# Vision tower on one core: edge filter in row tiles of 64 with both kernels side by side, halo rows split on GpSimd and stacked by transfers, eight banks in turn

## The chip, the cores and the metric

One core of one Trainium2 chip. The metric is the device time of one execution in microseconds, the median of several runs; lower is better. The kernel before takes 307.37 us (median of 3 runs, 306.79 to 307.87).

TensorE multiplies matrices into eight PSUM banks (PE in the profile, its weight loads PEld), VectorE (DVE), ScalarE (ACT) and GpSimd (POOL) work on elements, and SyncE (SP) issues transfers, as the other engines can. Each engine works through its own instructions in order and waits on semaphores for the others.

## The reference

Eight images of 3 x 256 x 256 become a tower of one layer. All is fp32.

```
gray  = einsum('bchw,c->bhw', x, (0.2989, 0.587, 0.114))
edges = conv3x3(gray, [scharr, scharr.T])            # SAME, zeros outside
h     = abs(edges).sum(over the two kernels) / 2     # [8, 256 rows, 256 columns]
n     = layernorm(h)
q, k, v = n @ Wq + bq, n @ Wk + bk, n @ Wv + bv      # 16 heads of 16
q, k  = q @ Wp, k @ Wp                               # per head
h     = h + softmax(q k' / 4) v                      # per image and head, 256 x 256 scores
n     = layernorm(h) * gamma + beta
h     = h + 0.5 * (silu(n @ w1 + b1) @ w2 + b2)      # w1, w2 dequantised from int32 with scales
```

## The kernel before

Every fp32 product is made of three fp32r matmuls: each operand is split into a high and a low part, and high x high, low x high and high x low are summed in a PSUM bank. So each stage has a copy that makes the high part (mostly ScalarE) and a subtraction that makes the low part (VectorE or GpSimd).

The images are worked on in four pairs (p = 0 to 3). An image's 256 rows are two tiles t of 128 rows. For a pair the tower does this:

- `gray_scale`, `gray_add`, `gray_high`, `gray_low`: the weighted sum of the three colours of image b and its two parts.
- `tok(p, i)`, i = 0 to 3: the edges of row tile `i // 2` with kernel `i % 2`, as matmuls of a banded 128x128 matrix with the gray rows, three for each of the three column shifts: nine of 512 columns (two images side by side). A tenth adds the halo: rows that belong to the neighbouring tile, kept for all images in `halo`.
- `edge`: ScalarE takes the absolute value of each bank, one kernel to `absd`, one to `hid`. `edges` on VectorE adds the two, `tok_moments` takes mean and variance, `tok_rstd` on GpSimd the inverse deviation, `tok_normalise` makes `xn`.
- `xt(p, kf)`: TensorE transposes `xn` into two banks; `xt_high` (ScalarE) and `xt_low` (VectorE) split it.
- `qkv(p, i)`, i = 0 to 5: four banks of q and k, two of v. ScalarE and VectorE split q and k (`qk_high`, `qkv_out`), SyncE stores them to DRAM (`store_qk`) and later loads them back per head (`load_qk`) into `qs` and `ks`. The scratch tiles of the tower (`gray`, `absd`, `halo_x`, the weight sources) lie in the memory of `qs` and `ks`.

The banks of `tok`, `xt` and `qkv` are taken in turn from banks 4 to 7 (list `turns`). Attention runs over 64 slots, a slot being a head pair of an image: `largest` (VectorE) takes the maxima of scores, `split_max` (GpSimd) splits them, `neg` (TensorE) transposes them, and so on; ten slots' maxima are made ahead, the first of them while the tower still works on pairs 2 and 3 (`HEAD_AT`). GpSimd prepares the FFN weights in spare slots from slot 6 on (`w1_step`), once SyncE has loaded them. The FFN is last.

The order on each engine is written out by hand; nothing schedules it. The loop over pairs stands once in each engine's block. For TensorE it is, in the order of before, `tok(p+1, 0)`, `tok(p+1, 1)`, `xt(p)`, `tok(p+1, 2)`, `tok(p+1, 3)`, `qkv(p, 0)` to `qkv(p, 5)`; the transposes of pair 3 stand inside the `qkv` of pair 2 (`XT_LAST`). SyncE's queue, in order, is: inputs, stores of pair 0, loads of pair 0, stores of pair 1, a wait for all of `edges` (since `absd` lies under `ks`/`qs`), half of pair 1's loads, stores of pair 2, the other half, stores of pair 3, a wait for two of these, and the FFN weights and scales:

```
            eng.wait_ge(s_glp, B - 2)
            eng.wait_ge(s_edges, NT * PAIRS)
            eng.wait_ge(s_wready, 5)
            stored(1, 0)
            for k in range(12):
                load_qk(1, 0, k)
```

Of the kernel before, what the change touches and what calls it, by code (L numbers as in the profile page):

```python
# [5 lines left out]
def vit_tower_kernel(nc, x, scharr, Wq, bq, Wk, bk, Wv, bv, Wp, ln_gamma, ln_beta,  # L6
# [13 lines left out]
    P = 128  # L20
# [14 lines left out]
    HALF = P // 2  # L35
    NCOL = HALF + SPLIT
# [3 lines left out]
    SLOTS = B * UNITS  # L40
    AHEAD = 10
# [34 lines left out]
    halo_m = at("halo_m", 17.9375, [P, NT, 3], fp32)  # L76
    halo_p = at("halo_p", 18, [P, NT, 2, 3], fp32)
    halo_w = at("halo_w", 18.0625, [P, NT * 2], fp32)
    halo_wh = at("halo_wh", 18.125, [P, NT * 2], fp32r)
    halo_wl = at("halo_wl", 18.1875, [P, NT * 2], fp32)  # L80
# [16 lines left out]
    band_h = at("band_h", 83.25, [P, 2, 3, P], fp32r)  # L97
    band_l = at("band_l", 86.25, [P, 2, 3, P], fp32r)
    halo = at("halo", 89.25, [96, B, E], fp32r)
    halo_b = at("halo_b", 97.25, [96, NT, 2, P], fp32r)  # L100
# [11 lines left out]
    masks = at("masks", 141.25, [P, 3, P], fp32)  # L112
# [5 lines left out]
    halo_x = at("halo_x", 143, [32, B, E], fp32)  # L118
# [4 lines left out]
    bandp = at("bandp", 163, [P, 2, 3, P], fp32)  # L123
    band = at("band", 167, [P, 3, P], fp32)
    band1 = at("band1", 173, [P, 3, P], fp32)
# [36 lines left out]
    with ctx:  # L162
# [9 lines left out]
        s_halo = sem("halo_loaded")  # L172
# [14 lines left out]
        s_bandp = sem("second_band_parts_ready")  # L187
        s_band1 = sem("second_band_ready")
        s_halo_h = sem("halo_high_ready")
        s_halo_l = sem("halo_low_ready")  # L190
# [4 lines left out]
        s_wready = sem("qkv_weights_ready")  # L195
# [11 lines left out]
        s_fill = [sem(f"filled{r}") for r in range(4)]  # L207
        s_free = [sem(f"freed{r}") for r in range(4)]
# [32 lines left out]
        XT_LAST = (PAIRS - 2, 3)  # L241
        turns = []
        for p in range(-1, PAIRS):
            if p + 1 < PAIRS:
                turns.extend(("tok", p + 1, i) for i in range(2 if p >= 0 else 4))
            if p >= 0:
                if p + 1 < PAIRS:
                    turns.extend(("xt", p, kf) for kf in range(KE))
                    turns.extend(("tok", p + 1, i) for i in (2, 3))
                for i in range(6):  # L250
                    turns.append(("qkv", p, i))
                    if (p, i) == XT_LAST:
                        turns.extend(("xt", p + 1, kf) for kf in range(KE))
        turn = {key: n for n, key in enumerate(turns)}
        last_turns = [[key for key in turns if turn[key] % 4 == r][-1] for r in range(4)]

        def turn_bank(key):
            return bank[4 + turn[key] % 4]

        def wait_filled(eng, key):  # L260
            n = turn[key]
# [1173 lines left out]
```

## Time and profile before

| What | us |
|---|---|
| median of 3 runs | 307.37 |
| the profiled execution | 307.51 |
| its span | 305.8 |
| PE, DVE, ACT, POOL busy over the span | 287.1, 214.6, 161.6, 131.2 |
| PE busy from 30 to 40 / 50 to 60 / 70 to 80 us | 10.00 / 10.00 / 10.00 |
| PE and DVE busy from 80 to 90 us | 10.00, 9.96 |
| PE busy from 140 to 180 us (attention) | 39.35 of 40 |
| POOL busy from 10 to 20 / 30 to 40 us | 2.29 / 1.69 |

```profile
PE   0499999999999999999999999999999999999996
DVE  8988874794799988888899888545845734632332
ACT  1491443533323487777786777768344344434440
POOL 7615141240200007953677581156859489500000
```

Each digit is the busy share in tenths of one of 40 slices of 7.6 us. The tower ends near 102 us, attention near 220, the FFN follows. The first two slices are the start, in which images and weights arrive.

### The profile page before, as it was taken

To read this page: it belongs to the slowest core of one execution; us is meant where nothing else is said; L and a number is where in the kernel's file an instruction comes from. 1 tells how busy PE (TensorE), PEld (TensorE's weight loads), DVE (VectorE), ACT (ScalarE), POOL (GpSimd) and SP (SyncE) were. 2 spreads that over 40 slices of the span, in tenths; PEclk is the share of its full clock that TensorE was granted. 3 is DMA by queue.
4 is the path that set the end of the run, shared out by engine and by line. 5 is a ranking of instruction groups with operands and counts; after the bars stand their busy time and mean duration, and the time that the engine had idled before them with its cause. 6 is when DMAs were issued, how large, how long until landed. Compare 5 with 4: busy or idle time off the path is not lost.

```text
span 305.8 us, 6170 instructions
## 1 busy us (share of the span) xinstructions
PE 287.1 (94%) x2280; PEld 224.7 (73%) x2280; DVE 214.6 (70%) x423; ACT 161.6 (53%) x304; POOL 131.2 (43%) x250
## 2 busy tenths in 40 slices
PE   0499999999999999999999999999999999999996
PEld 0378888887687766666666765666898998989976
DVE  8988874794799988888899888545845734632332
ACT  1491443533323487777786777768344344434440
POOL 7615141240200007953677581156859489500000
PEclk9999999999999999999999999999999999999999
DMA  6978017785388991578483000000000200200202
GB/s 206 331 208 257 2 70 267 184 237 207 87 260 269 303 319 56 156 204 273 138 179 107 4 3 2 0 2 2 0 1 2 70 2 0 69 2 0 71 0 69
DMA packets 26631, 35.30 MB, mean 115 GB/s; under 512 B 5082, under 2 KB 15594, under 8 KB 26602
## 3 DMA queue, kind: packets, MB, share of 16 engines
q1 hardware_dynamic: 26440, 34.77, 37.2%
q8 instruction: 18, 0.29, 0.4%
q10 hardware_dynamic: 162, 0.15, 0.2%
q14 instruction: 11, 0.09, 0.1%
HBM read 24.42 MB, written 10.49 MB: 114 GB/s over the span
## 4 chain that ended last, share of the span: by engine, by line
PE 73%; DVE 12%; DMA 5%; ACT 4%; issue 2%; POOL 1%; SPq 1%; ACTq 0%; DVEq 0%; POOLq 0%
PE bank L1142 46%; PE bank L1260 7%; PE bank L1212 6%; PE bank L1235 3%; PE bank L1240 3%; DVE negmax L848 3%; PE bank L1278 3%; DMA wscale<-in_L_ffn_fc_scales 2%; DMA qk_parts<-qk_l 2%; DVE gray L725 1%; PE bank L1164 1%; PE bank L1270 1%; PE bank L1286 1%; PE bank L1179 1%; ACT probs L1050 1%
## 5 line engine op out<-in xcount | busy, mean ns | idle before, releaser
L848 DVE TENSOR_REDUCE negmax<-bank 128x2 f32<-128x512 f32 x128 | 82.1, 684 | 6.1 <-PE bank L1212 5.8
L1050 ACT ACTIVATE probs<-bank 128x512 f32<-128x512 f32 x128 | 66.3, 603 | 27.8 <-PE bank L1240 27.8
L902 DVE TENSOR_TENSOR y_l<-yf,y_h 128x512 fp32r<-128x512 f32 x32 | 24.1, 754 | 38.6 <-ACT yf L1076 38.5
L1073 ACT ACTIVATE y_h<-bank,b1col 128x512 fp32r<-128x512 f32 x32 | 22.0, 687 | 47.7 <-PE bank L1142 47.6
L1142 PE MATMUL bank<-w_h,y_h 128*128 128x256 f32 x128 | 36.9, 289 | 1.1 <-DVE y_l L902 0.7
L1142 PE MATMUL bank<-w_l,y_h 128*128 128x256 f32 x128 | 36.2, 283 | 0.0
L1142 PE MATMUL bank<-w_h,y_l 128*128 128x256 f32 x128 | 36.2, 283 | 0.0
L1260 PE MATMUL bank<-probs,vals 128*32 128x256 f32 x512 | 34.3, 385 | 0.0
L1212 PE MATMUL bank<-ks,qs 48*128 48x256 f32 x256 | 32.2, 329 | 1.3 <-DVE negmax L848 0.7
L1212 PEld LDWEIGHTS bank<-ks,qs 48*128 48x128 f32 x256 | 19.3, 184 | 15.6 <-DVE negmax L848 6.6
L1142 PEld LDWEIGHTS bank<-w_h,y_h 128*128 128x128 f32 x128 | 24.4, 190 | 2.9 <-DVE y_l L902 1.9
L1240 PEld LDWEIGHTS bank<-qs,ks 48*128 48x128 f32 x256 | 24.2, 184 | 2.7
L1235 PE MATMUL bank<-negrow,pick 48*128 48x512 f32 x128 | 26.0, 402 | 0.0
L1142 PE MATMUL bank<-nt_h,w_h 128*128 128x512 f32 x64 | 25.8, 402 | 0.0
L1240 PE MATMUL bank<-qs,ks 48*128 48x256 f32 x256 | 25.5, 277 | 0.0
L1142 PE MATMUL bank<-nt_h,w_l 128*128 128x512 f32 x64 | 25.3, 395 | 0.0
L1142 PEld LDWEIGHTS bank<-w_h,y_l 128*128 128x128 f32 x128 | 24.4, 191 | 0.7
L1142 PE MATMUL bank<-nt_l,w_h 128*128 128x512 f32 x64 | 24.9, 390 | 0.0
L1142 PEld LDWEIGHTS bank<-w_l,y_h 128*128 128x128 f32 x128 | 24.4, 191 | 0.0
L553 POOL TENSOR_SCALAR negsplit<-negmax 128x8 fp32r<-128x8 f32 x32 | 5.9, 205 | 38.4 <-DVE negmax L848 35.4
L1076 ACT ACTIVATE yf<-bank,b1col 128x512 f32<-128x512 f32 x32 | 21.8, 683 | 0.0
L563 POOL TENSOR_TENSOR hid<-hid,att 128x256 f32<-128x256 f32 x16 | 12.1, 754 | 22.2 <-DVE att L859 22.2
(147 smaller groups left out, 613.0 us busy)
## 6 DMA issues: line engine op xcount, KB each, us to landing
xr<-in_x SPq DMA_DIRECT2D x8, 768.0 KB, 8.4
qs<-qk_parts SPq DMA_DIRECT2D x48, 128.0 KB, 3.1
ks<-qk_parts SPq DMA_DIRECT2D x48, 128.0 KB, 3.3
qk_parts<-qk_h SPq DMA_DIRECT2D x16, 256.0 KB, 3.1
qk_parts<-qk_l SPq DMA_DIRECT2D x16, 256.0 KB, 3.4
wraw<-in_L_ffn_fc_q SPq DMA_DIRECT2D x4, 512.0 KB, 4.6
wscale<-in_L_ffn_fc_scales SPq DMA_DIRECT2D x4, 512.0 KB, 6.7
out<-osb SPq DMA_DIRECT2D x16, 128.0 KB, 1.8
```

Source lines behind the costliest of these rows:

```text
L563: eng.tensor_tensor(h, h, att[:, u % 2, :], ALU.add).then_inc(s_h2, 1)
L848: eng.tensor_reduce(negmax[:, b % 2, u, v], entry_bank(key)[:, :].rearrange("p (t k) -> p t k", t=NT), AX.X, ALU.max, negate=True).then_in ...
L902: eng.tensor_tensor(y_l[:, p % 2, f], yf[:, n % 2], y_h[:, p % 2, f].bitcast(fp32), ALU.subtract).then_inc(s_y, 1)
L1050: eng.activation(probs[:, n % PBUF], p2[n % 4][:, :], ACT.Exp).then_inc(s_exp, 1)
L1073: eng.activation(y_h[:, p % 2, f], src, ACT.Silu, bias=b1col[:, f:f + 1])
L1076: eng.activation(yf[:, n % 2], src, ACT.Silu, bias=b1col[:, f:f + 1]).then_inc(s_silu, 1)
L1142: ins = eng.matmul(dst, l, r, start=first and i == 0, stop=i == len(steps) - 1 and not more_after)
L1212: ins = eng.matmul(entry_bank(("head", k, v))[:, t * N:(t + 1) * N], qs[rows, r, u, c + t * P:c + (t + 1) * P], ks[rows, r, u, c:c + N], s ...
L1235: eng.matmul(p2[(n + v) % 4][:, :].rearrange("p (t n) -> p t n", t=NT), pick[rows, u % 4:u % 4 + 1].broadcast_to([SPLIT, P]), negrow[rows, ...
L1240: ins = eng.matmul(p2[(n + v) % 4][:, t * N:(t + 1) * N], ks[rows, r, u, c + t * P:c + (t + 1) * P], qs[rows, r, u, c:c + N], start=False, ...
L1260: ins = eng.matmul(av[OROWS * j:OROWS * (j + 1), 0:N], vals[:, b, t, h * VW:h * VW + OROWS], probs[:, (4 * G + j) % PBUF, t * N:(t + 1) * ...
L1278: ins = eng.transpose(entry_bank(key)[:, g * P:(g + 1) * P], otr_of(4 * b + g)[:, t * P:(t + 1) * P], ident[:])
```

## The change

The three columns of weights of both kernels now stand side by side: a band matrix is 64 rows by 128 columns, 64 output rows of each kernel. A row tile of 128 is worked on as two halves of 64 rows, each with a bank of its own; the matmuls of the two halves alternate. Each half's bank has kernel 0 in its lower 64 partitions and kernel 1 in its upper ones, so ScalarE clears a bank with two copies of 64x512. There are now 18 matmuls and two for the halo in a tile, in place of 18 and two.

The halo consists of three kinds of rows (both sides of the middle of a tile, and the neighbouring tile's). They are loaded raw, colours unsummed, by images (`load_halo`); GpSimd sums and splits them (`halo_split`); transfers stack them three times, shifted by a column, with high and low parts, into 27 rows (`stack_halo`), four images at a time. Five of the first group's nine transfers are issued by ScalarE, the rest by SyncE.

Turns go over eight banks in the middle of the tower. TensorE transposes the identity 40 times at the start (`keep_busy`). The pieces move: `tok_normalise` from VectorE to ScalarE, `gray_high` of images 2 and 3 and the V weights' parts to GpSimd, the copies of `wtr` from ScalarE to VectorE; `tok_rstd` has four steps instead of two. The order in the loop over pairs changes on all engines.

```
-        XT_LAST = (PAIRS - 2, 3)
+        XT_LAST = (PAIRS - 2, 4)
...
+        fold_over, heads_begin = turn["qkv", 0, 0], turn["tok", PAIRS - 1, 0]
+        turn_at, nth, uses = {}, {}, [[] for r in range(8)]
+        for n, key in enumerate(turns):
+            if fold_over <= n < heads_begin:
+                r = (0, 1, 2, 3, 6, 7, 4, 5)[(n - fold_over) % 8]
+            else:
+                r = 4 + (n if n < fold_over else n - heads_begin) % 4
...
+        def load_halo(eng, g):
+            for r in range(3):
+                for t in range(NT):
+                    first = 32 * g + 4 * (NT * r + t)
+                    row = (t * P + HALF - 1, t * P + HALF, P - t)[r]
+                    eng.dma_start(halo_x[first:first + 4], x[4 * g:4 * g + 4, :, row, :]).then_inc(s_halo_x, 16)
+
+        def stack_halo(eng, g, dx, parts=range(3)):
+            lo, hi = max(0, 1 - dx), E - max(0, dx - 1)
+            for part in parts:
+                src = (halo_h, halo_h, halo_l)[part]
+                first = 9 * part + dx
+                eng.dma_start(halo[first:first + 7:3, g, :, :, lo:hi].rearrange("r t b w -> r (t b) w").bitcast(fp32),
+                              src[32 * g:32 * g + 24, lo + dx - 1:hi + dx - 1].bitcast(fp32)).then_inc(s_halo[g], 16)
...
 SyncE:
             load_x(0)
-            load_x(1)
+            load_halo(eng, 0)
+            for b in range(1, 4):
+                load_x(b)
...
+            eng.wait_ge(s_border, 7)
+            eng.wait_ge(s_halo_g, 1)
+            stack_halo(eng, 0, 2)
+            stack_halo(eng, 0, 1, (2,))
+            load_halo(eng, 1)
...
                 load_x(b)
+                if b == 5:
+                    eng.wait_ge(s_halo_g, 2)
+                    for dx in range(3):
+                        stack_halo(eng, 1, dx)
...
 GpSimd:
+                eng.tensor_scalar(nmean_a[:, js], mv[:, js, 0], -1.0, 0.0, ALU.mult, ALU.add)
                 link(eng.tensor_scalar(vareps[:, js], mv[:, js, 1], EPS, 1.0, ALU.add, ALU.mult))
-                eng.tensor_tensor(rstd[:, js], vareps[:, js], mhalf[:, js], ALU.pow).then_inc(s_rstd, 1)
+                link(eng.tensor_tensor(rstd[:, js], vareps[:, js], mhalf[:, js], ALU.pow))
+                eng.tensor_tensor(shift_a[:, js], nmean_a[:, js], rstd[:, js], ALU.mult).then_inc(s_rstd, 1)
...
+            gray_high(2)
             gray_low(2)
+            gray_high(3)
             gray_low(3)
+            eng.wait_ge(s_wld, 16 * (NT + 1))
+            link(eng.tensor_scalar(wqk_h[:, :, 2 * E:], wv_src[:], 1.0, 0.0, ALU.mult, ALU.add))
+            eng.tensor_tensor(wqk_l[:, :, 2 * E:], wv_src[:], wqk_h[:, :, 2 * E:].bitcast(fp32), ALU.subtract).then_inc(s_wvready, 1)
             tok_rstd(0, 0)
             tok_rstd(0, 1)
...
+            halo_split(1)
...
 ScalarE:
+            def edge(p, t):
+                for half in range(2):
+                    key = ("tok", p, 2 * t + half)
+                    rows = slice(HALF * half, HALF * (half + 1))
+                    wait_filled(eng, key)
+                    eng.activation(hid[rows, p, t].rearrange("p b e -> p (b e)"), turn_bank(key)[0:HALF, :], ACT.Abs)
+                    if p >= 1 and half == 0:
                         eng.wait_ge(s_edges, NT * (p - 1) + t + 1)
+                    eng.activation(absd[rows, t], turn_bank(key)[HALF:P, :], ACT.Abs).then_inc(freed(key), 1)
...
+            stack_halo(eng, 0, 0)
+            stack_halo(eng, 0, 1, (0, 1))
+            for t in range(NT):
+                edge(0, t)
+            tok_normalise(0, 0)
+            edge(1, 0)
+            tok_normalise(0, 1)
+            edge(1, 1)
...
 TensorE:
+                for dx in range(3):
+                    for i, (w, g) in enumerate(((band_h, gray_h), (band_l, gray_h), (band_h, gray_l))):
+                        for half in range(2):
+                            rows = slice(HALF * half, HALF * (half + 1))
+                            eng.matmul(dst[half], w[rows, dx].rearrange("p k j -> p (k j)"), g[rows, p % 2, t, :, dx:dx + E],
+                                       start=dx == 0 and i == 0, stop=False)
...
+            keep_busy(30, bank[0])
+            eng.wait_ge(s_gray, 1)
+            keep_busy(10, bank[0])
```

Three places of the order, each of pair 1. First TensorE, between the edges of pair 2 and the `qkv` of pair 1. Before, with `xn` the normalised pair 1 that is transposed:

```order
L1142 MATMUL bank<-gray_l,band_h 128x512
L1164 MATMUL bank<-halo,halo_b 128x512
L1179 MATMUL bank<-ident,xn 128x128 [waits xn_ready,freed2]
L1179 MATMUL bank<-ident,xn 128x128 x3
L1179 MATMUL bank<-ident,xn 128x128 [waits freed3]
L1179 MATMUL bank<-ident,xn 128x128 x3
L1142 MATMUL bank<-gray_h,band_h 128x512 [waits freed0]
L1142 MATMUL bank<-gray_h,band_l 128x512
```

The same place now:

```order
L1225 MATMUL bank<-gray_l,band_h 128x512 x2
L1238 MATMUL bank<-halo,halo_b 128x512 [waits halo_stacked1]
L1238 MATMUL bank<-halo,halo_b 128x512
L1254 MATMUL bank<-ident,xn 128x128 [waits xn_ready,freed0]
L1254 MATMUL bank<-ident,xn 128x128 x3
L1254 MATMUL bank<-ident,xn 128x128 [waits freed1]
L1254 MATMUL bank<-ident,xn 128x128 x3
L1207 MATMUL bank<-xt_h,wqk_h 128x512 [waits freed1,freed0,freed2]
L1207 MATMUL bank<-xt_h,wqk_l 128x512
```

The transposes were followed by two more banks of edges; now the first `qkv` follows at once, and waits until both transpose banks have been read (`freed0`, `freed1`).

Second VectorE, in pair 1, between the first and the second `qk_l`. Before (L794 is `edges`, L724 and L725 are `gray_add`, L798 and L801 the moments):

```order
L794 TENSOR_TENSOR hid<-hid,absd 128x512 [waits freed1,freed0]
L798 BN_STATS stats<-hid 128x6 [waits edges_added]
L801 BN_AGGR mv<-stats 128x2 [waits vector_chain]
L813 TENSOR_SCALAR xn<-hid,mv,rstd 128x256 [waits filled3,rstd_ready]
L838 SCALAR_TENSOR_TENSOR qk_l<-bank,qk_bias,qk_h 128x512 [waits high_part_ready]
L724 SCALAR_TENSOR_TENSOR gray<-xr,gray 128x512 [waits gray_begun]
L725 SCALAR_TENSOR_TENSOR gray<-xr,gray 128x512 [waits vector_chain]
```

Now, from the first `qk_l` (L908) on; L804 and L805 are `gray_add(7)`, L873 is `edges(2, 1)`:

```order
L908 SCALAR_TENSOR_TENSOR qk_l<-bank,qk_bias,qk_h 128x512 [waits high_part_ready]
L804 SCALAR_TENSOR_TENSOR gray<-xr,gray 128x512 [waits gray_begun]
L805 SCALAR_TENSOR_TENSOR gray<-xr,gray 128x512 [waits vector_chain]
L873 TENSOR_TENSOR hid<-hid,absd 128x512 [waits freed6,freed3]
L877 BN_STATS stats<-hid 128x6 [waits edges_added]
L880 BN_AGGR mv<-stats 128x2 [waits vector_chain]
```

The last edge addition of the pair stood ahead of `qkv`'s output and of the second gray addition; now it stands behind both.

Third ScalarE, in pair 1, from the first `qk_high` on. Before (L1041 is `qk_high`, L1024 `edge`, L1008 `gray_high`, L1001 `gray_scale`):

```order
L1024 ACTIVATE absd<-bank 128x512 [waits edges_added,filled0]
L1024 ACTIVATE hid<-bank 128x512 [waits filled1]
L1008 ACTIVATE gray_h<-gray 128x2x256 [waits filled1,gray_summed]
L1001 ACTIVATE gray<-xr 128x512 [waits gray_low_by_pool,x_loaded3]
L1041 ACTIVATE qk_h<-bank,qk_bias 128x512 [waits qk_stored0,filled2]
```

Now (L1107 `qk_high`, L1078 and L1081 `edge`, L1070 `gray_high`, L1063 `gray_scale`):

```order
L1107 ACTIVATE qk_h<-bank,qk_bias 128x512 [waits qk_stored0,filled2]
L1078 ACTIVATE hid<-bank 64x512 [waits filled3]
L1081 ACTIVATE absd<-bank 64x512 [waits edges_added]
L1078 ACTIVATE hid<-bank 64x512 [waits filled6]
L1081 ACTIVATE absd<-bank 64x512
L1070 ACTIVATE gray_h<-gray 128x2x256 [waits filled7,gray_summed]
L1063 ACTIVATE gray<-xr 128x512 [waits gray_low_by_pool,x_loaded3]
L1107 ACTIVATE qk_h<-bank,qk_bias 128x512 [waits qk_stored1,filled7]
```

The edge copies, the gray high part and the scaling of the next image stood ahead of the first `qk_high`; now they stand behind it, and the edge copies are four instead of two.

## Rows read from the trace of the kernel before

**Rows 1.** Chain that ended last, 98 to 125 us: start, duration, what

```profile
108.56 6.79 DMA wscale<-in_L_ffn_fc_scales
...
117.93 1.29 POOL w1full L613
...
119.75 0.37 POOL negsplit L556 x2
...
120.25 0.40 PE bank L1270 x2
```

**Rows 2.** Timeline of SyncE's queue: start, duration, engine, line, operation

```profile
79.58 3.75 SPq L389 DMA_DIRECT2D qs<-qk_parts  x6
...
107.22 0.83 SPq L401 DMA_DIRECT2D wraw<-in_L_ffn_fc_q  x2
```

**Rows 3.** Timeline of VectorE, last edge addition; in brackets its wait before

```profile
78.82 0.69 DVE L794 TENSOR_TENSOR hid<-hid,absd 128x512 f32<-128x512 f32 x1 [1.77 <-ACT hid L1024]
```

**Rows 4.** Timeline of TensorE, start and tower

```profile
11.22 1.94 PE L1331 MATMUL bank<-ident,wsrc 128*128 128x128 f32 x8 [11.22 <-DMA wsrc<-in_L_attn_Wk]
...
33.41 1.04 PE L1179 MATMUL bank<-ident,xn 128*128 128x128 f32 x8
...
38.99 0.39 PE L1142 MATMUL bank<-xt_h,wqk_h 128*128 128x512 f32 x1
...
47.92 0.40 PE L1142 MATMUL bank<-gray_h,band_h 128*128 128x512 f32 x1
...
67.07 0.40 PE L1142 MATMUL bank<-gray_h,band_h 128*128 128x512 f32 x1
```

**Rows 5.** Chain that ended last, first 24 us

```profile
9.53 0.72 DVE gray L724
...
12.33 0.65 ACT gray_h L1008
13.00 0.70 DVE gray_l L730
13.84 4.18 PE bank L1142 x9
...
21.54 2.09 PE bank L1142 x9
```

**Rows 6.** Timeline of TensorE in attention, matmuls of 48 rows

```profile
144.28 0.39 PE L1235 MATMUL bank<-negrow,pick 48*128 48x512 f32 x2
144.51 0.40 PE L1240 MATMUL bank<-qs,ks 48*128 48x256 f32 x4
```

**Rows 7.** Timeline of ScalarE

```profile
3.10 5.07 ACTq L992 DMA_DIRECT2D halo_x<-in_x  x6
...
13.87 1.28 ACT L1012 ACTIVATE halo<-halo_x 32x512 fp32r<-32x512 f32 x2 [0.90 <-DMA halo_x<-in_x]
...
34.11 1.08 ACT L1033 ACTIVATE xt_h<-bank 128x512 fp32r<-128x512 f32 x2
...
99.93 0.38 ACT L1057 ACTIVATE negrow<-bank 112x256 fp32r<-112x256 f32 x1 [1.58 <-PE bank L1270]
```

**Rows 8.** The tile of the images: durations in ns, min/median/max

```profile
L725 DVE SCALAR_TENSOR_TENSOR gray<-xr,gray x8: 691/692/1470, 10.3 to 62.7; 128x512 f32<-128x512 f32 x8
```

**Rows 9.** Timeline of GpSimd

```profile
64.92 1.28 POOL L536 TENSOR_TENSOR gray_l<-gray,gray_h 128x512 fp32r<-128x512 f32 x1 [1.30 <-ACT gray_h L1008]
...
80.67 0.19 POOL L542 TENSOR_SCALAR vareps<-mv 128x2 f32<-128x2 f32 x1 [2.56 <-DVE mv L801]
80.94 0.70 POOL L543 TENSOR_TENSOR rstd<-vareps,mhalf 128x2 f32<-128x2 f32 x1
...
120.57 1.06 POOL L620 TENSOR_SCALAR w_h<-w1full 128x1024 fp32r<-128x1024 f32 x1
```

**Rows 10.** Transfers by line: count, size, us from issue to landing

```profile
qs<-qk_parts SPq DMA_DIRECT2D x48, 128.0 KB, 3.1
```

More of the change, by code:

```diff
@@ L40, in vit_tower_kernel @@
     SLOTS = B * UNITS
+    WARM = 18
     AHEAD = 10
@@ L356, in wait_room @@
                     wait_drained(eng, last[0])
+            for r in sorted({ebank[key] for key in keys if not before[key]}):
+                wait_read(eng, uses[r][-1])
         LN_AT = (SLOTS - 32, SLOTS - 10)
@@ L758, in _ @@
+            gray_add(0)
+            gray_low(0)
+            gray_add(1)
+            gray_low(1)
+            halo_bands()
+            gray_add(2)
+            for op in range(2):
+                eng.wait_ge(s_wt, op + 1)
+                eng.tensor_copy(wtr[:, op], bank[op][:, :]).then_inc(s_wtc, 1)
+            gray_add(3)
             eng.wait_ge(s_ident, 1)
@@ L1118, in _ @@
                     qk_high(p, i)
+                    if i == 0 and more and p:
+                        edge(p + 1, 1)
+                    if i == 0 and p + 2 < PAIRS:
+                        gray_high(2 * p + 4)
+                        gray_scale(2 * p + 5)
+                    if i == 1 and more:
+                        tok_normalise(p + 1, 0)
                     if i == 1 and p + 2 < PAIRS:
                         gray_high(2 * p + 5)
+                if more:
+                    tok_normalise(p + 1, 1)
             neg_rows(0, 1)
@@ L1143, in product, with tok @@
                 return ins
-            def tok(p, i):
-                t, k = i // 2, i % 2
-                key = ("tok", p, i)
-                wait_freed(eng, key)
-                if p == 0 and i == 1:
-                    eng.wait_ge(s_band1, 1)
-                if i == 0:
+            def tok(p, t):
+                keys = [("tok", p, 2 * t + half) for half in range(2)]
+                for key in keys:
+                    wait_freed(eng, key)
+                if t == 0:
                     if p == 0:
@@ L1325, in _ @@
             eng.wait_ge(s_ident, 1)
+            keep_busy(30, bank[0])
+            eng.wait_ge(s_gray, 1)
+            keep_busy(10, bank[0])
+            eng.wait_ge(s_band, 1)
+            eng.wait_ge(s_border, 7)
+            for t in range(NT):
+                tok(0, t)
             eng.wait_ge(s_wsrc, 32)
@@ L1371, in _ @@
                     behind("qkv", p, i)
+                    if i == 0 and more and p:
+                        tok(p + 1, 1)
+                        behind("tok", p + 1, 3)
                     if (p, i) == XT_LAST:
```

364 lines of the change are left out of this document (170 added, 194 removed).

## The prediction, made before the changed kernel was run

> **What bounds the kernel now.** I read the chain of waits first, near the start of attention, because a change in the first third only counts if something behind it does not absorb it. There the reader is to see that TensorE is held by a transfer [rows 1]: the scales of the first FFN layer land at 115.35 us, GpSimd works on them until 119.2, only then splits a maximum (done at 120.12), and TensorE takes its transposes at 120.25. The next view is the transfer queue of SyncE [rows 2]. Its loads of pair 1 are issued at 79.58, and 24 loads and 16 stores follow without a pause until it issues the FFN loads at 107.22. What released 79.58 is VectorE's last edge addition, `edges(3, 1)`, which runs 78.82 to 79.51 [rows 3]. So one date of the tower goes through to the end at one for one: when `edges(3, 1)` ends. Attention behind 120 us keeps TensorE busy in 39.35 of 40 us (table of the profile section) and gives nothing back.
>
> Then TensorE's timeline of the tower [rows 4]: the first `qkv` of pair 0 starts at 38.99, the edges of pair 2 at 47.92, those of pair 3 at 67.07, with hardly a gap. Before, a tower pair is TensorE's own work.
>
> **The change part by part.** *Matmuls.* An edge bank was nine matmuls and one for the halo, 2.09 us for nine [rows 5], so 9.3 us for a pair's four banks. Now each of the 18 products of a row tile uses 64 rows, and two of them, on rows 0 to 63 and 64 to 127, stand next to each other. Nearest rows: two 48-row matmuls of 512 columns at 144.28 are followed at 144.51 by the next ones [rows 6], so two cost one, 0.23. A tile is then 9 x 0.23 = 2.1, plus two halo matmuls in the same rows (0.47): 2.57, and 5.1 for a pair instead of 9.3. That takes 4.2 x 4 = 16.7 us of work off TensorE. Bounds: none of it (two cost two) and all of it.
>
> *What gets later.* Nothing is left behind `xt` to hide its copies. Before, two edge banks (4.7 us) stood between `xt` and `qkv`. Now `qkv` follows `xt` at once for pairs 1 and 2, and ScalarE must clear the edges first. A bank half is 64x512, so a tile needs four copies instead of two. Rows of ScalarE say that fewer partitions save nothing: two 32x512 copies took 1.28 and two 128x512 copies 1.08 [rows 7], so a tile's four copies are 2.1. From the start of `tok(p+1, 0)` to the first `qkv`: 2.5 until both halves are read from, 2.1 of edges, 1.1 for `xt_high`, 0.65 for the last `xt_low`, and hand-overs, 0.3: 6.7. TensorE works 3.5 of these.
>
> *Pair 0's start.* VectorE loses the halo weights ahead of the first image, but builds both kernels' bands in 18 half-wide steps; I let its first gray addition move from 9.53 [rows 5] to 8.7. Then high and low part follow each image before the next is summed: twice 0.72 + 0.69 + 0.65 + 0.70 [rows 5, 8] = 5.5 and hand-overs, 14.4 against 13.84. TensorE has run 40 transposes until then. The clock shows in the pace: eight transposes took 1.94 at 11.22 and 1.04 at 33.41 [rows 4], nine matmuls 4.18 at 13.84 and 2.09 at 21.54 [rows 5]. I take the first edges at the faster pace, done at 18.7. Their halo waits for the stack. ScalarE issues five transfers for it after `gray_scale(3)` at 15.0, 0.85 each as its six before [rows 7], until 19.2; a transfer of the same queue hardware lands 3.1 after its issue, the median of 48 [rows 10]. So the halo matmuls start at 21.5. The bounds of this landing are 20.5 and 25: of ScalarE's old six the last was issued by 8.17 and its reader began at 13.87.
>
> From 21.5 the chain is ScalarE: edges(0,0) and (0,1), 4.1, to 26.2. GpSimd now has two more high parts, the V weights and four small operations per `rstd` instead of two. Low parts cost 1.28 each and slow when VectorE reads two inputs, a high part about 0.55 (half of 1.06), `rstd` about 1.6 (0.19, 0.70 and two more) [rows 9]. They end with `rstd(0, 0)` at 28.3. Then ScalarE: normalise 0.75 (0.38 for 256 columns), edges(1,0) 2.1, normalise, edges(1,1): 34.1. VectorE adds (0.69), takes moments (1.1, the distance from 79.51 to GpSimd's 80.67), and two low parts (1.3). First `qkv` of pair 0 at 37.5, before 38.99: 1.5 earlier. The VectorE moves are covered: its four old normalisations of pair 0 go, two copies of `wtr` come.
>
> *Pair 0 to pair 2.* `qkv` of pair 0 takes 8.4 in its six parts (TensorE is not held, all banks are free): `tok(2, 0)` at 45.9, before 47.92. Its halo needs group 1, split on GpSimd by 34 and stacked by nine transfers on SyncE, by 43: hidden, with 3 us to spare. `qkv` of pair 1 at 45.9 + 6.7 = 52.6, before 58.12.
>
> *The new wait.* Here the order costs what the matmuls saved. `tok(2, 1)` starts 1.4 later, at 54.0. VectorE's `gray_add(7)` stands ahead of `edges(2, 1)` and waits for `gray_scale(7)`, which stands behind the four copies and `gray_high(6)` on ScalarE. GpSimd's two low parts stand behind `rstd(2, 1)`. So from 54.0: 4.65 to the last copy, 1.15 for `gray_high(6)` and `gray_scale(7)`, 1.45 for `gray_add(7)` (two steps of 0.69 [rows 8]), 0.75 edges, 1.1 moments, 1.6 `rstd`, 2.6 for two low parts: 13.3, and `tok(3, 0)` starts at 67.3. TensorE has 2.6 + 7.0 us of work, so it stands for 3.7. Before, the same matmul started at 67.07 with no wait. The gain of 5.5 is gone here.
>
> *Pair 3.* 67.3 + 6.7 = 74.0 for `qkv(2, 0)`, 1.4 for it, 0.45 for head 1, 4.65 until `tok(3, 1)` is copied, 0.7: `edges(3, 1)` ends at 81.2, before 79.51. That is 1.7 later, and so are the FFN scales and TensorE's 120.25. The other way into attention, VectorE's maxima, comes to the time of before or up to 1 earlier and is covered.
>
> The sum is made on the profiled execution, 307.51 us (its span 305.8 and 1.7 around it), 0.14 above the median of 307.37: 307.5 + 1.7 = 309.2, less 0.1 for the median: **309.1 us**.
>
> **The rivals.** *A, faster: the start is shorter than I make it.* If GpSimd's added work is hidden and the halos land at once, only TensorE's work counts: 14.4 + 4.2 edges, 0.9 and 0.9 transposes and halos, 1.8 and 0.8 folding, 5.1 edges of pair 1 = 28.1, then 5.2 of copies, sum, moments and low parts: first `qkv` at 33.3, 4.2 earlier than forecast. `edges(3, 1)` would end at 77.0, 2.5 before the old date: 304.9. It turns at 35.8: below that the kernel is faster. For it: every GpSimd price is from an engine that shared its time with VectorE. Against: ScalarE's order holds whatever GpSimd does.
>
> *B, slower: the first edges run at the low pace.* Then 14 matmul steps cost 0.2 more, 2.8 us, of which the stack hides 0.8 by its own date: 311. For it: in the trace the pace changed only after 6 us of real matmuls; nothing shows that transposes of the identity raise it.
>
> *C, slower: the clock falls in the new gaps.* TensorE now stands about 4 us before the first `qkv` and 3.7 before `tok(3, 0)`; in the tower of before it never stood that long. One fall costs what the start paid, (4.18 - 2.09) / 9 = 0.23 for each of some twelve matmuls: 2.8 us, 312 for one and 315 for two. The Trainium skill says as much (TensorE: Matmul & The Clock Gate, "HAM oscillation — how this bites in real kernels"): gaps in which TensorE idles put it back to the slow clock. By that rule the time would be C's; the trace agrees that TensorE begins slow after idling, and has no gap inside the tower to judge the rest.
>
> *D, slower: the ScalarE transfers land at 25* because the images saturate the transfer engines: 3.5 later, 312.6. For it: the reader at 13.87; against: with the images ahead of the weights the engines have less to do by 15.
>
> *E: the change does not do what it says*, two row tiles run one after the other. Each tile on the chain costs 2.1 more, six of them: 321. Rows 6 speak against it.
>
> **How the numbers follow.** The forecast has a chance of 0.36 with 307.5 to 311, since seven prices of about 0.3 stand in the chain; A 0.31, B 0.14, C 0.09, D 0.08, E 0.02. The range is 304.5 (A at its end) to 313 (C once, D). Under 0.3% (0.9 us) this kernel's measurement does not tell a change from none. A gives 0.29 of faster and 0.02 of no change; the forecast 0.01 of faster, 0.16 of no change and 0.19 of slower; B to E are slower, 0.33: faster 0.30, same 0.18, slower 0.52.
>
> **What would show it.** In the changed profile: idle TensorE before the first `qkv` of pair 0 (about 4 us), of pairs 1 and 2 (3 each) and before `tok(3, 0)` (3.7, released by GpSimd's low part); halo matmuls at 21.5; SyncE's loads of pair 1 at 81.2 instead of 79.58; TensorE held by GpSimd's split at about 122. The chain should name ScalarE's half copies, absent before. I am wrong if `tok(3, 0)` starts before 65, which would mean a start or a GpSimd queue shorter than priced; or if attention no longer waits for the FFN scales at all, so that the date of `edges(3, 1)` does not count.

## The result, and the profile after

| | before | after |
|---|---|---|
| median | 307.1 us (306.79 to 307.87) | 325.65 us (324.18 to 327.92) |
| ratio | | 1.061, 95% interval 1.058 to 1.064 |
| profiled execution, its span | 307.51, 305.8 | 327.92, 326.2 |
| mean granted clock of TensorE | 1.0 | 0.948 |

The change makes the kernel 6% slower. Forecast were 309.1 and a range of 304.5 to 313.0: the sign was right (slower had been given 0.52), the size was not. The profiled execution of the changed kernel is the longest of its four, 2.3 above their median, so differences between traces come out larger than those between medians. The kernel before was measured again beside each group of experiments, with medians of 306.8 to 307.3. Ratios are formed from executions in the faster of the chip's two states alone, so a ratio can differ a little from the quotient of two medians.

First the page of the changed kernel, busy tenths in 40 slices of 8.2 us, and the granted clock:

```profile
PE   5498398696698999599999999999999999999996
DVE  6868463552649798468888988863692563552422
PEclk9989769797699999959999999999999999999999
```

The clock row has dips in slices 3, 5, 6, 8, 10, 11 and 18, and most stand in or beside a dip in PE. The windows of the same trace put numbers to them (us from the start and length, then busy us and instructions of TensorE, its weight loads, VectorE, ScalarE and GpSimd; the third number from the end is the granted clock):

```profile
10.00:20.00 10.00, 5.94 (x36) 5.34 (x38) 7.42 (x29) 3.05 (x5) 4.76 (x8) 0.83 0.77 236
30.00:40.00 10.00, 5.26 (x30) 3.45 (x28) 5.57 (x16) 8.52 (x15) 7.74 (x18) 0.80 0.34 113
40.00:50.00 10.00, 8.54 (x31) 7.00 (x32) 6.37 (x11) 5.01 (x9) 3.62 (x6) 0.69 0.45 128
60.00:70.00 10.00, 10.00 (x46) 7.21 (x45) 3.22 (x8) 5.11 (x9) 2.10 (x4) 0.83 0.78 199
80.00:90.00 10.00, 7.09 (x32) 4.97 (x34) 5.22 (x11) 4.14 (x7) 1.28 (x4) 0.67 0.01 2
```

In the stretch of 60 to 70 PE is busy all the time, and still it works less (46 instructions): a busy share does not show at which pace. The timeline of TensorE does (start, duration, operation, in brackets the wait before it and who ended it). These rows answer to [rows 4]:

```profile
15.37 0.68 PE L1225 MATMUL bank<-gray_h,band_h 64*128 64x512 f32 x2 [4.03 <-DVE gray_l L810]
...
35.98 1.92 PE L1254 MATMUL bank<-ident,xn 128*128 128x128 f32 x8 [2.64 <-ACT xn L1088]
41.46 0.77 PE L1207 MATMUL bank<-xt_h,wqk_h 128*128 128x512 f32 x1 [3.56 <-DVE xt_l L891]
42.02 0.63 PE L1207 MATMUL bank<-xt_h,wqk_l 128*128 128x512 f32 x1
42.45 0.63 PE L1207 MATMUL bank<-xt_l,wqk_h 128*128 128x512 f32 x1
...
46.52 0.39 PE L1207 MATMUL bank<-xt_h,wqk_h 128*128 128x512 f32 x1
46.74 0.39 PE L1207 MATMUL bank<-xt_h,wqk_l 128*128 128x512 f32 x1
...
59.58 0.48 PE L1207 MATMUL bank<-xt_h,wqk_h 128*128 128x512 f32 x1 [3.33 <-DVE xt_l L891]
...
76.21 0.50 PE L1225 MATMUL bank<-gray_h,band_h 64*128 64x512 f32 x2 [3.37 <-POOL gray_l L603]
...
85.11 0.76 PE L1207 MATMUL bank<-xt_h,wqk_h 128*128 128x512 f32 x1 [2.90 <-DVE xt_l L891]
```

Read the distance between starts, not the durations, which overlap: after the wait at 41.46 the `qkv` matmuls start 0.43 apart, after 46.3 they start 0.23 apart. That is the pace of 1.2 GHz and then of 2.4 GHz. By the granted clock, read in windows of 0.1 to 0.5 us, the tower has five slow stretches: 15.5 to 18.9, 36.0 to 46.2, 59.9 to 63.3, 77.0 to 80.2 and 83.8 to 90.6. The last begins inside the wait that ends at 85.11, the others at the end of a wait shown or at most 0.8 behind it. The second goes on through the wait that ends at 41.46, so that wait and the one before it share one fall. The rest of the path is as forecast, and later. The last edge addition, SyncE's loads, the FFN scales, GpSimd's split and TensorE, in this order [rows 1 to 3]:

```profile
94.73 0.69 DVE L873 TENSOR_TENSOR hid<-hid,absd 128x512 f32<-128x512 f32 x1 [4.01 <-ACT absd L1081]
...
95.49 3.77 SPq L431 DMA_DIRECT2D qs<-qk_parts  x6
...
121.93 1.26 SPq L443 DMA_DIRECT2D wraw<-in_L_ffn_fc_q  x2
...
133.23 1.05 POOL L679 TENSOR_SCALAR w1full<-wraw 128x1024 f32<-128x1024 int32 x1 [6.43 <-DMA wscale<-in_L_ffn_fc_scales]
...
138.02 0.40 PE L1347 MATMUL bank<-ident,negsplit 128*112 128x128 f32 x2 [3.58 <-POOL negsplit L625]
...
139.69 0.63 PE L1312 MATMUL bank<-negrow,pick 48*128 48x512 f32 x2
140.12 0.63 PE L1317 MATMUL bank<-qs,ks 48*128 48x256 f32 x4
```

The span grew by 20.4: 15.9 at the end of `edges(3, 1)` (79.51 to 95.42), less 1.2 in SyncE's queue (27.64 to 26.44), 2.6 more for the landing of the scales (6.79 to 9.43), and 2.6 for the slow stretch behind TensorE's wait at 138.02; 0.5 is spread.

### The profile page after: what moved, and what is told of

Its sections match the earlier page's. It is cut to its first block, busy times and chain, and to the rows that moved or that the text cites. A ratio compares the mean times of both kernels' runs of the same rounds, so it can differ in the third digit from the quotient of the medians.

```text
span 326.2 us, 6324 instructions
## 1 busy us (share of the span) xinstructions
PE 290.1 (89%) x2320; PEld 224.4 (69%) x2320; DVE 205.0 (63%) x425; ACT 173.4 (53%) x328; POOL 140.4 (43%) x274
## 4 chain that ended last, share of the span: by engine, by line
PE 61%; DVE 11%; SPq 7%; ACT 7%; DMA 5%; POOL 4%; issue 4%; ACTq 0%; DVEq 0%; POOLq 0%
PE bank L1207 31%; PE bank L1337 7%; PE bank L1289 6%; PE bank L1225 5%; SPq L431 4%; PE bank L1312 3%; PE bank L1317 3%; DMA wscale<-in_L_ffn_fc_scales 3%; PE bank L1355 3%; SPq L421 2%; DVE negmax L918 2%; ACT absd L1081 2%; ACT hid L1078 1%; POOL gray_l L603 1%; PE bank L1347 1%
## 5 line engine op out<-in xcount | busy, mean ns | idle before, releaser
L1337 PE MATMUL bank<-probs,vals 128*32 128x256 f32 x512 | 35.1, 393 | 0.0
L1289 PE MATMUL bank<-ks,qs 48*128 48x256 f32 x256 | 33.1, 336 | 2.0 <-DVE negmax L918 1.4
L1289 PEld LDWEIGHTS bank<-ks,qs 48*128 48x128 f32 x256 | 20.1, 192 | 16.8 <-DVE negmax L918 7.3
L1207 PE MATMUL bank<-xt_h,wqk_h 128*128 128x512 f32 x32 | 15.1, 473 | 10.7 <-DVE xt_l L891 10.7
```

Source lines behind the costliest of these rows:

```text
L1207: ins = eng.matmul(dst, l, r, start=first and i == 0, stop=i == len(steps) - 1 and not more_after)
L1289: ins = eng.matmul(entry_bank(("head", k, v))[:, t * N:(t + 1) * N], qs[rows, r, u, c + t * P:c + (t + 1) * P], ks[rows, r, u, c:c + N], s ...
L1337: ins = eng.matmul(av[OROWS * j:OROWS * (j + 1), 0:N], vals[:, b, t, h * VW:h * VW + OROWS], probs[:, (4 * G + j) % PBUF, t * N:(t + 1) * ...
```

## The experiments

Two theories for the later `edges(3, 1)`: TensorE's clock falls in the waits and the slow matmuls behind them are the loss, or the waits are themselves the loss. And one rival on where the waits come from: the tiles (half-wide copies, halo rows) instead of the loop order. A kernel's date is here the end of its `edges(3, 1)`.

**Filling the waits.** Transposes of the identity stand in TensorE's order where it idled:

```
-            keep_busy(10, bank[0])
+            keep_busy(42, bank[0])
...
+                    keep_busy((28, 25, 22)[p], turn_bank(key))   # before qkv(p, 0)
+                    keep_busy(20, turn_bank(key))                # before xt(0)
+                    keep_busy(26, turn_bank(keys[0]))            # before tok(3, 0)
+                    keep_busy(28, entry_bank(key))               # before neg(2, 0)
```

> The changed kernel, with TensorE's idle stretches filled by transposes of the identity: 42 instead of 10 at the start, 20 before xt(0), 28, 25 and 22 before the first qkv of pairs 0, 1 and 2, 26 before tok(3, 0), 28 before the negated maximum of image 2 in attention. Nothing else moves. Theory 1 (TensorE's clock falls in these gaps, and the slow stretches behind them are the greater part of the loss): the granted clock of 20:60, 70:90 and 130:150 returns to 1.00, edges(3, 1) ends at about 86 instead of 95.4, TensorE leaves the split in attention 2.6 us sooner, together about -12, to 312 to 315. Theory 2 (order and waits alone set the end, the clock only follows; or transposes do not hold it): 324 to 328, no change or slower by transposes that stand in the way.

Measured: 318.01 (317.34 to 320.71), ratio to before 1.035 (1.030 to 1.040). The clock stays at 1.00 from 20 us on. 7.6 faster, but not the 12 expected: the first edges began at 18.07 instead of 15.37, while their input was there at 16.04 in this execution; for about 2 us it was the 42 transposes that held them. So the counts were fitted (28, 16, 18, 24).

> The first filled kernel again, with the transposes counted so that they end where the waits end: 28 instead of 42 at the start, 16 instead of 20 before xt(0), 18 instead of 26 before tok(3, 0), 24 instead of 28 in attention. In the first one the edges of pair 0 began at 18.07 instead of 15.37, because 42 transposes lasted longer than the wait, and its time was 318.0. If the rest of what was missed to 313.6 was this overshoot: 315 to 316.5 now. If the clock is worth no more than the 7.6 already seen: 317.5 to 318.5.

Measured: 316.84 (316.01 to 317.74), ratio 1.032 (1.030 to 1.035), between the two expectations. The date is 87.87 instead of 95.42. TensorE's timeline of this kernel, to be held against 41.46 and 42.02 above:

```profile
41.44 0.47 PE L1207 MATMUL bank<-xt_h,wqk_h 128*128 128x512 f32 x1 [1.42 <-DVE xt_l L891]
41.74 0.39 PE L1207 MATMUL bank<-xt_h,wqk_l 128*128 128x512 f32 x1
41.97 0.40 PE L1207 MATMUL bank<-xt_l,wqk_h 128*128 128x512 f32 x1
```

The first `qkv` starts at the same time, 41.44 and 41.46. Only the pace behind it differs. So the slow clock behind the filled waits is 8.8 of the 18.6 us lost (325.65 - 316.84). Nearly all of the rest is not clock. One slow stretch is left in this trace, 16.0 to 19.5 behind a wait of 2.07, and by the traces compared below it costs 0.8; the two executions with a mean clock of 1.000 took 316.01 and 316.68, the two with 0.995 317.0 and 317.74.

**One wait opened again,** to price a single fall: the fitted kernel with `(28, 0, 22)`.

> The fitted fill (316.84) without the 25 transposes before the first qkv of pair 1, so that one gap of 3.3 us is open again and all others stay filled. It prices one fall of the clock: in the changed kernel's trace the stretch from there to the next qkv part lasted 6.02 (59.58 to 65.60) and in the fitted fill 4.49 (57.35 to 61.84), 1.5 more. If gap and clock go together and the tower passes the delay on: 318.0 to 318.8 and a granted clock near 0.83 in that stretch alone. If falls come from something else than the gap before them: 316.5 to 317.2.

Measured: 318.01 (317.56 to 319.05), 1.2 more than with all filled, at the lower edge of what was expected. TensorE's timeline of this kernel:

```profile
56.49 0.77 PE L1207 MATMUL bank<-xt_h,wqk_h 128*128 128x512 f32 x1 [3.34 <-DVE xt_l L891]
57.05 0.63 PE L1207 MATMUL bank<-xt_h,wqk_l 128*128 128x512 f32 x1
57.48 0.63 PE L1207 MATMUL bank<-xt_l,wqk_h 128*128 128x512 f32 x1
...
59.71 0.39 PE L1227 MATMUL bank<-gray_h,band_l 64*128 64x512 f32 x2
...
62.31 0.50 PE L1207 MATMUL bank<-xt_h,wqk_h 128*128 128x512 f32 x1
```

and its clock, with one window of the tower below 1.00:

```profile
40.00:50.00 10.00, 9.38 (x56) 8.20 (x58) 7.72 (x13) 6.04 (x11) 3.44 (x4) 1.00 0.54 153
50.00:60.00 10.00, 6.66 (x36) 4.42 (x34) 4.32 (x10) 4.54 (x8) 2.09 (x4) 0.83 0.92 322
80.00:90.00 10.00, 9.54 (x54) 6.80 (x55) 6.69 (x17) 5.30 (x9) 1.67 (x7) 1.00 0.03 9
```

From 56.49 to 62.31 is 5.82; with transposes ahead the same stretch took 4.49. One wait of 3.3 us costs 1.3 behind its end. The fall belongs to the wait, and nothing else was changed. The date moved by less, 88.30 against 87.87: the start of this execution happened to run at the upper pace (1.00 from 10 to 20 us, where the fitted fill has 0.83), and its first `qkv` came at 40.62 instead of 41.44. So the firm price is the 1.3 of the stretch; the 1.2 between the medians holds such differences of the start too.

**Tiles and order apart.** The changed tiles, halos and banks in the loop order of before (on TensorE `tok(p+1, 1)` behind `xt(p)` instead of behind `qkv(p, 0)`, the same on ScalarE and VectorE):

```
                     for kf in range(KE):
                         xt(p, kf)
+                    tok(p + 1, 1)
+                    behind("tok", p + 1, 3)
...
-                    if i == 0 and more and p:
-                        tok(p + 1, 1)
-                        behind("tok", p + 1, 3)
```

> The changed kernel's tiles (two row tiles of 64, halos raw and stacked, eight banks) with the loop order of the kernel before: tok(p+1, 0), xt(p), tok(p+1, 1), qkv(p) on TensorE, the edges and moments of the second half ahead of qkv on ScalarE and VectorE. Theory 1 (the order makes the gaps, and the gaps the slow clock): the second tok stands again between xt and qkv, edges(3, 1) ends at 73 to 79, and the time is 300 to 307, below the kernel before. Theory 3 (the tiles themselves cost: four half-wide copies, the switch of the tile's rows, the halo chain of GpSimd): gaps stay before qkv, edges(3, 1) ends at 85 or later, 313 to 325.

Measured: 307.68 (306.34 to 309.81), ratio 1.000 (0.997 to 1.003). The date is 79.01, at the late end of what was expected, and the time just above it: the order gives back all that was lost, and the new tiles gain nothing. The clock still falls twice at the start of this kernel (0.66 from 10 to 20, 0.69 from 30 to 40). And the reverse, the old tiles, halos and four banks in the new order:

> The kernel before (edge banks of nine 128-row matmuls, banks in turns of four, its own halo) with the changed kernel's loop order alone: for pair 1 both halves of the edges ahead of xt(0), for pairs 2 and 3 the second half behind the first part of qkv, on TensorE, ScalarE and VectorE. With e2_old_order this makes a square of tiles and order. If the order is the cause, whatever the tiles: gaps of 2 to 4 us appear before the first qkv of each pair and before tok(3, 0), the clock falls in some of them, and the time is 318 to 330. If the order hurts only with half-wide copies: 307 to 312.

Measured: 323.16 (320.41 to 326.31), ratio 1.050 (1.044 to 1.056), date 93.13. Its waits of TensorE up to 150 us (who waited for whom, us, times, longest):

```profile
PE bank L1154 <- DVE xt_l L824: 6.9, 4, 2.9
PE bank L1154 <- DVE qk_l L841: 3.5, 1, 3.5
```

In the kernel before, TensorE waited for `xt_l` nowhere in the tower. The four medians:

| | old order | new order |
|---|---|---|
| old tiles | 307.1 | 323.2 |
| new tiles | 307.7 | 325.65 |

The order costs 16 with the old tiles (13.5 to 17.2 by the interval of the ratio) and 18 with the new ones. The 0.6 and 2.5 of the tiles are not clear of the noise: in the new order the four times with the old tiles alone spread over 5.9.

**One part of the order.** `gray_high(6)` and `gray_scale(7)` ahead of the four copies of `tok(2, 1)` on ScalarE, `gray_low(6)` ahead of `rstd(2, 1)` on GpSimd:

```
+                    if i == 0 and p + 2 < PAIRS:
+                        gray_high(2 * p + 4)
+                        gray_scale(2 * p + 5)
                     if i == 0 and more and p:
                         edge(p + 1, 1)
-                    if i == 0 and p + 2 < PAIRS:
-                        gray_high(2 * p + 4)
-                        gray_scale(2 * p + 5)
```

> The changed kernel with one part of its order alone undone: ScalarE does gray_high(6) and gray_scale(7) ahead of the four copies of tok(2, 1), and GpSimd gray_low(6) ahead of rstd(2, 1). If the chain through VectorE's gray_add(7) is what held tok(3, 0) (3.4 us of idle TensorE at 76.2), tok(3, 0) starts at 73 to 74, its clock stays up, and the time is 319.5 to 322.5. If another wait stands behind it (the lows behind the moments): 324 to 326.

Measured: 320.47 (317.81 to 322.27), 5.2 less than the changed kernel, as expected. TensorE's timeline of it, where the wait of 3.37 at 76.21 stood:

```profile
72.87 0.50 PE L1225 MATMUL bank<-gray_h,band_h 64*128 64x512 f32 x2
...
80.26 0.58 PE L1207 MATMUL bank<-xt_h,wqk_h 128*128 128x512 f32 x1 [2.90 <-DVE xt_l L891]
```

The wait is gone, and `tok(3, 0)` starts 3.3 earlier and keeps its pace. This is the fastest of the four executions and the one with the highest mean clock (0.968 against 0.952 to 0.962); how the others ran is not in a trace.

**The wait in attention.** GpSimd's `spare` slots begin at 10 instead of 6, so its steps on the FFN scales stand behind the first split maxima; in the changed kernel, and in the one before:

```
-            spare = [s for s in range(6, SLOTS - 8) if s % 8 in (0, 2, 3, 4, 6, 7)]
+            spare = [s for s in range(10, SLOTS - 8) if s % 8 in (0, 2, 3, 4, 6, 7)]
```

> The changed kernel with the first six slots of GpSimd's spare list taken away, so that its steps that wait for the scales of the first FFN layer stand behind the first split maxima of attention. If TensorE's hold of 3.6 us at 138 and the slow stretch behind it (2.6) hang on that order: 319 to 320.5. If the transfers hold attention in another way, or the end is set elsewhere: 325 to 326. It also says whether the date of edges(3, 1) still reaches the end: with this wait gone the late tower counts only by TensorE's own work.

> The kernel before with the same edit of GpSimd's spare list. There TensorE waited only 0.1 to 0.2 us for the split at 120.25. Expected 306.8 to 307.3, no change; more than 0.5 faster would mean that the date of edges(3, 1) had more weight in the kernel before than its chain of waits shows.

Measured, in the changed kernel: 321.9 (321.75 to 322.31), 3.75 less, between the two expectations; between the profiled executions it is 5.6 (326.2 to 320.6 of span). The wait for the split and the slow stretch are gone, the date is the same (95.66). That the medians show 1.9 less than the traces comes from the changed kernel's profiled execution, 2.3 above its median; what made it longer stays open. In the kernel before: 306.44 (305.83 to 307.35), ratio 0.997 (0.995 to 0.999), 0.9 less than the 307.31 beside it, and more than the 0.5 that was given as the mark. The traces don't show that its date had more weight: of the 1.1 between their spans 0.88 lies ahead of `edges(3, 1)` (78.63 against 79.51), where this edit changes nothing. With the scales out of the way in both kernels, 15.5 of the loss are still there (321.9 against 306.44).

**Clock and order together.** The old order with the start and `xt(0)` filled:

> The changed tiles in the old loop order (307.7), with its two idle stretches filled too: 28 instead of 10 transposes at the start, 24 before xt(0). Nothing else moves. In its trace the first edges ran 10 pairs and the edges of pair 1 eight pairs at the slow pace. If clock and order add up: 303.5 to 305.5, and the difference to the filled kernel with the new order (11 to 12 us) is what the order costs without the clock. If the start's slow pace is hidden behind the transfer of the halo rows and ScalarE's copies: 306.5 to 307.7.

Measured: 307.25 (306.17 to 310.82), ratio 1.002 (0.998 to 1.005): nothing. The windows of 10 to 20 and 30 to 40 us have clocks of 0.83 and 0.84, up from 0.66 and 0.69, and the date moved by 0.7. In this order ScalarE's copies and the halo rows are later than the matmuls, so a slow matmul there costs next to nothing.

**The best version.** The same (28 transposes at the start) with 10 before `xt(0)`, `spare` from 10, and on GpSimd:

```
-            link(eng.tensor_scalar(wqk_h[:, :, 2 * E:], wv_src[:], 1.0, 0.0, ALU.mult, ALU.add))
-            eng.tensor_tensor(wqk_l[:, :, 2 * E:], wv_src[:], ...).then_inc(s_wvready, 1)
             tok_rstd(0, 0)
             tok_rstd(0, 1)
+            link(eng.tensor_scalar(wqk_h[:, :, 2 * E:], wv_src[:], 1.0, 0.0, ALU.mult, ALU.add))
+            eng.tensor_tensor(wqk_l[:, :, 2 * E:], wv_src[:], ...).then_inc(s_wvready, 1)
```

> The same with 10 transposes before xt(0), and two edits on GpSimd: the split of the V weights (2.5 us at 27.95) behind rstd(0, 0) and rstd(0, 1) instead of ahead of them, and the first six slots of the spare list gone, so that the FFN scales hold no split maximum. xt(0) should start near 32.5 instead of 34.81 and PE should not wait for the split (1.3). Theory: 300.5 to 302.5, faster than both kernels. Rival: the loads of SyncE and attention's own work take over as the bound: 304 to 306.

Measured: 303.95 (303.7 to 304.14), ratio 0.990 (0.989 to 0.992): 1% below the kernel before and 6.7% below the changed one, though between the two expectations. The date is 75.90. Timelines of TensorE and GpSimd in it:

```profile
21.49 1.14 PE L1227 MATMUL bank<-halo,halo_b 27*128 27x512 f32 x4 [0.61 <-DMA halo<-halo_h]
...
26.93 0.19 POOL L605 TENSOR_SCALAR nmean_a<-mv 128x2 f32<-128x2 f32 x1 [1.78 <-DVE mv L876]
...
31.56 1.09 PE L1245 MATMUL bank<-ident,xn 128*128 128x128 f32 x8 [1.94 <-ACT xn L1079]
```

`rstd(0, 0)` now waits for VectorE's moments instead of standing behind a weight split; in the changed kernel its first step ran at 29.63. `xt(0)` starts at 31.56, 2.4 earlier than in the kernel with the same order and fill (33.95). Not all of it is the split: in this execution the first edges also ran at the upper pace (1.00 from 10 to 20 us, 0.83 there), which in the two filled kernels of the new order was worth 0.8 (first `qkv` at 40.62 and 41.44). The kernel of the copy order below has the same GpSimd edit and a slow start, and its `xt(0)` starts at 32.37: 1.6 for the split and 0.8 for the pace.

**The new order with all of this mended.**

> The changed kernel's own loop order with everything else mended that the runs so far point at: the fitted transposes in the gaps (2 only before xt(0), 6 before tok(3, 0), none in attention), gray_high(6), gray_scale(7) and gray_low(6) first, the V split behind rstd(0, 1), the first six slots of the spare list gone. In the fitted fill edges(3, 1) ended at 87.87; 2.4 less for the V split and about 2.6 for the gray order give 82.9, against 75.9 in the old order with the same repairs (303.95). If the waits of the loop order (qkv right behind xt, ScalarE's four copies bare) are what is left: 309 to 311.5, still slower than the kernel before. If the order itself costs nothing once clock and gray work are right: 304 to 306.

Measured: 308.88 (308.04 to 309.35), ratio 1.005 (1.003 to 1.007), just below what was expected, date 82.60, clock 1.00 throughout. It is 4.9 behind the best version, and its date 6.7. What is left in its trace is `qkv` right behind `xt`: ahead of the three first `qkv` parts TensorE does 28, 25 and 22 transposes of the identity and still waits 1.43, 0.62 and 0.51. So 16.8 us of the loss are repaired in TensorE's own loop order, but below the kernel before it comes only in the old one.

**The order of ScalarE's copies** (both to `hid`, then both to `absd`), on the best version:

> The best kernel so far (303.95) with ScalarE's four copies of a tile in another order: both halves to hid, then both to absd, instead of hid, absd, hid, absd. The copies of 64x512 ran 0.60 to 0.61 apart with no overlap, where pairs of 128x512 ran 0.54 apart. If the distance comes from the change of source and target rows between neighbours, the four take 2.2 instead of 2.45 and edges(3, 1) ends 0.5 to 1.5 earlier: 302.7 to 303.5. If it belongs to a copy out of a bank on 64 rows: 303.7 to 304.3, no change.

Measured: 304.18 (303.58 to 304.3), ratio 0.989 (0.986 to 0.993), no change against 303.95. ScalarE's timeline of it:

```profile
22.86 1.19 ACT L1069 ACTIVATE hid<-bank 64x512 f32<-64x512 f32 x2 [6.83 <-PE bank L1230]
24.06 1.21 ACT L1075 ACTIVATE absd<-bank 64x512 f32<-64x512 f32 x2
```

Two in a row to the same target still take 1.19 and 1.21. The distance of 0.60 belongs to such a copy, whatever stands next to it.

## Why the prediction was wrong, step by step

- *What bounds the kernel.* Right for the changed kernel: its chain runs from `edges(3, 1)` through SyncE's queue and the scales to TensorE. For the kernel before, one for one was more than its chain shows. There the chain is TensorE's own matmuls until 97.64, goes on over ScalarE and VectorE, and meets SyncE's queue only at the stores of pair 3:

```profile
97.66 0.70 ACT qk_h L1041
...
98.39 0.75 DVE qk_l L838
...
101.30 0.43 SPq L379
...
102.27 4.86 DMA qk_parts<-qk_l
```

  The queue was busy from 79.58 until then as well, so the two ways ended together: a later date is passed on, an earlier one need not be. Nor is the queue the only way by which a late tower reaches the end, since 15.5 of the loss stand with the scales out of it. Over all these kernels the span less the date lies between 224.0 and 230.8, while the date moves by 20.5 (75.19 to 95.66): the date marks how far the tower has come, whichever way leads on.
- *The matmuls.* Right: pairs on 64 rows start 0.233 apart. Rival E (one after the other) is out.
- ***Pair 0's start, and the distance of 6.7.* The step that failed.** "I take the first edges at the faster pace" was carried on to every stretch: the sum has four waits of TensorE of 3 to 4 us and no slow matmul behind any of them. The mechanism stood there as rival C, with one or two falls and a chance of 0.09, although the forecast itself listed the waits. The runs: the clock was low behind all of them, and fell at the start, before `xt(0)` and in attention too. In the tower this was 7.55 us of date (95.42 - 87.87), and 0.8 more at the start. Held against the fitted fill, stretch by stretch: nothing up to the first `qkv`, since both have the slow start, 2.2 behind it (41.46 to 52.20 against 41.44 to 49.96), 1.3 in pair 1, 4.0 from `tok(3, 0)` to the date (76.21 to 95.42 against 72.63 to 87.87). In attention it was 2.6. A fall cost less than the 2.8 of rival C, but C had one or two of them. The Trainium skill (TensorE: Matmul & The Clock Gate, "HAM oscillation — how this bites in real kernels"), which says that idle gaps put TensorE back to the slow clock, had been cited for this and given too little weight; the trace agrees, with 0.67 to 0.85 in the windows behind these waits.
- *The other sizes*: they failed too, and the clock alone would not have put the time in the range: with the waits filled it is 316.84, above 313. The date of that kernel is 87.87 against 81.2. The first `qkv` came at 41.44 instead of 37.5: 0.8 of it is the slow start, the four copies of a tile took 2.45 instead of 2.1, `rstd(0, 0)` ended at 31.15 instead of 28.3 because the V split ahead of it held it, `xn` took 1.09 instead of 0.75. `tok` to `qkv` took 7.4 instead of 6.7 twice, and the 13.3 from `tok(2, 1)` to `tok(3, 0)` were 13.7 (58.90 to 72.63). From `qkv(2, 0)` to the date it was 7.8 instead of 7.2. Sum: 3.9 + 1.4 + 0.4 + 0.6, and 0.4 of small change and rounding: 6.7.
- *The new wait* was right in place and cause: GpSimd's low part released `tok(3, 0)`, and taking the gray work out of ScalarE's way removed it.
- *The covered edits.* One was not covered: the V split on GpSimd. The stack landed when forecast, 21.5 (the wait that ends at 21.49 above); in the changed kernel the matmuls came at 22.3, since the slow first edges ended later. So rival D (25) is out, and B (slow first edges) came true and cost 0.8.
- *Rival A* (start shorter, 304.9) had the most weight of the rivals, 0.31, and the start gave it nothing: apart from the landing of the stack its prices were too low.
- *Behind the date* the forecast took 1.7 for 1.7. The scales then landed 2.6 slower and the wait at 138.02 had its own fall. In the kernels whose chain shows this landing it took 6.6 to 9.4; what sets it stays open.

Together, between spans: forecast 307.5, + 6.7 sizes (0.8 of them the slow start), + 7.55 clock in the tower, + 2.6 clock and + 2.6 landing in attention, less 1.2 of SyncE's queue: 325.8, measured 326.2.

## What to carry to other kernels

When a change shortens or moves matmuls, ask what they hid: here the second edges between `xt` and `qkv` hid ScalarE's and VectorE's work on `xt`, and without them it became a wait, with the old tiles as with the new. Price each new wait of TensorE twice, once as the wait and once as the slow stretch behind it (1.3 where one of 3.3 us was opened alone), and count all of them before the mechanism gets its chance. If a wait can't be ordered away, transposes of the identity in it cost nothing as long as they end before the input arrives (first `qkv` at 41.44 and 41.46); they help only where TensorE is what others wait for (307.68 and 307.25 in the old order).

## What the runs showed of the hardware

- Behind TensorE's waits of 2.64, 2.90, 3.33, 3.37, 3.56, 3.58 and 4.03 us in the changed kernel, and 2.94 and 3.52 with the old tiles, the pace fell to that of 1.2 GHz; behind single waits of 1.04, 1.42, 1.67 and 1.90 it did not. Shorter waits close to each other are not safe: it fell behind 1.94 and 1.44 with eight transposes between them in the best version (slow from 34.2 to 37.6), and behind 0.76 and 1.43 in the old order with fill (slow from 36.8 to 40.3), but not behind 0.75 and 1.44 in the copy-order kernel. After 2.07 or 2.08 at the start, with the same transposes and matmuls up to there, both were seen: a clock of 1.00 from 10 to 20 us in three traces (one wait opened, best version, new order mended), 0.83 in three (fitted fill, old order with fill, copy order). So the length of a wait alone does not decide it. The fall can come late: in the changed kernel 0.8 behind the wait's end, in the old tiles with the new order 1.3 (wait to 73.72, slow from 75.0).
- The granted clock does not show every slow stretch: in the kernel before it is 1.00 from the start on, but the matmuls from 13.84 to 19.95 start 0.43 apart, the pace of 1.2 GHz.
- Transposes of the identity count as work: with them alone in the waits of pairs 0 to 3 the clock stayed at 1.00. They also bring the upper pace by themselves. In the changed kernel nothing but transposes ran before this row, and ten take 0.13 each, where eight at the slow pace took 1.92 at 35.98:

```profile
10.03 1.31 PE L1244 MATMUL bank<-ident 128*128 128x128 f32 x10 [0.43 <-DVE gray L805]
```

  The Trainium skill (TensorE: Matmul & The Clock Gate, "Part 4: PE-mode transpose") says of transposes that they don't engage the fast clock; here the measurement decides against it, for fp32 transposes of the identity.
- A copy by ScalarE of 64x512 out of a bank holds the next up for 0.60 to 0.62 in both orders tried; the copies of 128x512 of the kernel before for 0.50 (`hid` at 58.32, the next instruction at 58.82). Half the partitions cost no less, but more.
- Two halo matmuls on 27 rows, after 64-row ones, took 0.65 until the next matmul; a 96-row halo matmul with the old tiles took 0.23 to 0.24, so two would take 0.47. Whether the 27 rows or the switch from 64 does it was not separated.
